# Router-table writes spread over POOL's steps, weight pieces at other places, six score banks for the last batch

## The chip, the cores and the metric

The kernel runs on one core of one Trainium2 chip. The metric is the device time of one execution in microseconds (us). The engines are called PE (matrix multiplications), DVE (vector), ACT (scalar), POOL (GpSimd) and SP (which only issues transfers). They run side by side, each through its own list of instructions in order, and wait for each other by semaphores.

## The reference

A Flamingo block on 32 batches of 112 tokens, width 256. First a cross attention whose queries come from the normed tokens x, and whose keys and values come from 375 normed context rows and the 112 normed tokens themselves (487 keys, 16 heads of 64):

```python
q, kv = lat @ Wq, concat([ctx_norm, lat]) @ Wkv
attn = softmax(q k^T / 8);  x = x + tanh(g_xattn) * (attn @ v) @ Wout
```

Then a mixture of 8 experts on the layer-normed result, two experts a token, hidden width 1024:

```python
gate = softmax(xn @ gate_w);  two best, their scores normed to sum 1
h = gelu(xn @ w1[e] + b1[e]);  y = h @ w2[e] + b2[e]
x = x + tanh(g_ffn) * (score0 * y0 + score1 * y1)
```

## The kernel before

Products are made of float16 (or float32r) halves: a number is split into a high and a low part, and three products of parts stand for one. ACT writes the high part, DVE or POOL the low one.

**The attention part** is one long software pipeline over steps t (`STEPS`, from -24 to 275). A step works on one pair of heads; a batch has 8 steps (`NP`), so batch b starts at t = 8b, and j = t % 8 is the place in the batch. `PAIRS` is 256. In step t PE makes, where t is even, the scores of pairs t and t+1 (L1125) into four banks `scores_ps`, then the K and V projections of pair t+8 into the two banks `proj_ps` (L1107), then the product with V of pair t-4 (L1156). Before the scores of step t it waits until all pairs before t are exponentiated. DVE takes each score's row minimum (`shifted_minimum`, L864), ACT the exponential (L639, function `exponential`), which waits until POOL is done with the pair two before, since `p_f` has two buffers. ACT then makes the high part of p (`p_high_of`, L648) and POOL the low part (`p_low_of`, L510). SP transposes p by DMA. POOL does o_f (L530) and o_low (L516) for the attention output too.

**The later stages** of a batch (output projection `out` L1176, residual and statistics `x2`, `rstd2`, `xn`, router logits, `top` for MAX8, and by groups of batches `hot`, `share`, `prefix`, `rank`, `entry`) hang on fixed steps counted from the batch's first one (`USUAL`, `LATE` for batch 29, `EARLY` for 30 and 31). `GROUPS` says which batches are ranked together: 8, 8, 8, 4, 2, 1 and 1. When a group is ranked (`rank_entries`), POOL writes for each batch and each of a token's two experts one row set into a table in DRAM, an indirect DMA (L587). `entries_at` gives one batch, two writes, to each step from the group's `entry` step on. The first group's writes are in steps 89 to 96, the second's in 153 to 160, the third's in 217 to 224 and the fourth's in 249 to 252.

**Weight pieces.** The experts' weights are 32 pieces ("units") of 512 KB, four an expert. A piece is loaded by SP (`load_unit`), split by ACT (`unit_high_of`, L667) and DVE (`unit_low_of`, L906). `SPLITS` puts pieces 0 to 22 in steps 250, 252, 254 and 256 to 275, `BEFORE_TILES` has 23 to 25, `TILE_SPLITS` 26 to 31 in iterations -2 to 3 of the tile loop. `LOADS` loads the piece four further one step after each split, since a load waits until its slot's former piece is split. b2 (1 MB) is loaded in step 260.

**Before the tiles** DVE computes from the counts which tile belongs to which expert (`table_row`, sets `row_known`); POOL waits for this and for all table writes, then reads the table (L593); PE turns it, DVE copies it, and POOL gathers the first rows (L599).

**The tile loop** has 35 tiles of 256 rows. Iteration t makes on PE the hidden layer of tile t+1 (L1256), the transposes of tile t+2 (L1266), and y of tile t (L1280). The hidden layer of tile n < 8 waits until 4(n+1) pieces are split. DVE splits the hidden values (L1052, L1054), splits the transposed x (L1066, L1068), makes y (L1076), and then splits its weight pieces of this iteration. Last, sums are copied to the output.

Of the kernel before, what the change touches and what calls it, by code (L numbers as in the profile page):

```python
# [82 lines left out]
GROUPS = ((0, 8), (8, 16), (16, 24), (24, 28), (28, 30), (30, 31), (31, 32))  # L83
# [16 lines left out]
def entries_at(t):  # L100

    return [first + t - step_of("entry", last - 1) for first, last in GROUPS if 0 <= t - step_of("entry", last - 1) < last - first]
# [18 lines left out]
def program(nc, x, ctx_in, g_x, g_f, ln_m_g, ln_m_b, ln_l_g, ln_l_b, wq, wkv, wout, gate_w, w1, b1, w2, b2, out):  # L121
# [4 lines left out]
    with ExitStack() as st:  # L126
# [195 lines left out]

        def subtracted(b):

            return POOL_BASE + POOL_COUNT * (b + 1)
# [49 lines left out]
        def _(sp):  # L375
# [37 lines left out]
            for t in STEPS:  # L413
# [44 lines left out]
                if t in LOADS:  # L458
                    load_unit(LOADS[t])
# [4 lines left out]
            for u in LAST_LOADS:  # L464
# [11 lines left out]
        def _(pool):  # L476
# [42 lines left out]
            for t in STEPS:  # L519
# [60 lines left out]
                for ob in entries_at(t):  # L580
# [5 lines left out]
                    for k in range(TOPK):  # L586
                        pool.indirect_dma_start(table.rearrange("r (n w) -> (r n) w", w=2), bass.IndirectOffsetOnAxis(ap=place_i[0:LQ, ob, k:k + 1], axis=0),  # L587
                                                entry[0:LQ, ob, k], None).then_inc(entered, 16)
# [37 lines left out]
        def _(act):  # L626
# [6 lines left out]
            def exponential(p, h):  # L633
# [5 lines left out]
                act.activation(p_f[0:LQ, p % 2, h, 0:LK], scores_ps[n][0:LQ, 0:LK], ACT.Exp, bias=shift[0:LQ, p // 2 % 2, n:n + 1], scale=-1.0,  # L639
# [29 lines left out]
            for t in STEPS:  # L669
# [55 lines left out]
                if t in SPLITS:  # L725
                    unit_high_of(SPLITS[t])
# [5 lines left out]
            for t in range(-2, TILES + 1):  # L732
# [23 lines left out]
                if t in TILE_SPLITS:  # L756
                    unit_high_of(TILE_SPLITS[t])

        @block.vector
        def _(dve):  # L760
# [100 lines left out]
            def shifted_minimum(p, h):  # L861
                n = 2 * (p % 2) + h
                dve.wait_ge(scores_done, 2 * p + h + 1)
                dve.tensor_scalar(passed[0:LQ, n, 0:LK], scores_ps[n][0:LQ, 0:LK], P_SHIFT, None, ALU.add, ALU.min,  # L864
# [43 lines left out]
            for t in STEPS:  # L908
# [103 lines left out]
                if t in SPLITS:  # L1012
                    unit_low_of(SPLITS[t])
# [297 lines left out]
```

## Time and profile before

| | |
|---|---|
| runs of the kernel before | 1851.1, 1853.73, 1851.03 us, median 1851.1 |
| the profiled execution | 1851.1 us, its span 1849.4 us |
| mean granted clock of PE | 0.967 of full speed |
| busy: PE, DVE, ACT, POOL | 90%, 71%, 65%, 68% of the span |
| PE's clock in 40 slices of the span | 0.9 or more in nearly all, 6, 5 and 8 tenths in slices 30 to 32 |

Slices are 46 us wide. The attention part ends in slice 29, the slices 30 and 31 hold the last stages of the last batches and the reading of the table, and the tile loop fills the rest.

### The profile page before, as it was taken

The page shows a single profiled execution, that of the slowest core. Times are in us where ns is not written, and L with a number is a line of the kernel's source. Part 1 is how long each engine was busy: PE and PEld are TensorE (multiplying, and loading weights), DVE is VectorE, ACT ScalarE, POOL GpSimd, SP SyncE. Part 2 cuts the span into 40 slices and gives each one's busy share as a digit, 9 for nine tenths or more (in the row PEclk, how much of TensorE's full clock was granted, in tenths as well). Part 3 has the DMA queues.
Part 4 walks back from the last instruction along what each step waited for, and adds up shares of the span by engine and source line. Part 5 has one row for each costly group of instructions (what it writes and reads, how often), then busy time and mean ns, then how long its engine had stood idle before and what let it go on. Part 6 is the DMA issues. An engine that isn't in the chain of part 4 may idle for free. (4 is left out here: it accounts for less than half of the span.)

```text
span 1849.4 us, 42314 instructions
## 1 busy us (share of the span) xinstructions
PE 1670.0 (90%) x15044; PEld 1168.0 (63%) x15044; DVE 1307.3 (71%) x3059; ACT 1200.6 (65%) x2732; POOL 1259.7 (68%) x1350
## 2 busy tenths in 40 slices
PE   1899999999989999998999999999851899999995
PEld 0456666666655666665566666556541799999994
DVE  4677787777766877776677778677665676666662
ACT  2587777777767787776787777677753444444442
POOL 5377777877788877778877777886673355445542
PEclk9999999999999999999999999999965899999998
DMA  4177767677657677676676767555788133323334
GB/s 146 36 140 137 148 143 146 139 148 144 140 113 139 137 150 149 139 142 111 136 145 137 143 142 141 108 113 106 161 203 244 47 50 53 50 47 50 52 51 103
DMA packets 597544, 223.37 MB, mean 121 GB/s; under 512 B 535202, under 2 KB 587984, under 8 KB 596892
## 3 DMA queue, kind: packets, MB, share of 16 engines
q1 hardware_dynamic: 581804, 202.18, 52.1%
q0 software_dynamic: 15536, 18.49, 6.4%
q8 instruction: 126, 2.06, 0.5%
q14 instruction: 78, 0.64, 0.1%
HBM read 71.39 MB, written 20.76 MB: 50 GB/s over the span
## 5 line engine op out<-in xcount | busy, mean ns | idle before, releaser
L510 POOL TENSOR_TENSOR p_parts<-p_space,p_parts 112x487 f16<-112x487 f32 x512 | 559.8, 1117 | 167.3 <-ACT p_parts L648 166.8
L639 ACT ACTIVATE p_space<-scores_ps,shift 112x487 f32<-112x487 f32 x512 | 338.6, 665 | 46.4 <-POOL p_parts L510 44.5
L864 DVE TENSOR_SCALAR_CACHE_REDUCE passed<-scores_ps 112x487 f16<-112x487 f32 x512 | 308.6, 660 | 26.3 <-PE scores_ps L1125 25.9
L694 ACT ACTIVATE k_hi<-proj_ps 128x488 fp32r<-128x488 f32 x256 | 148.0, 578 | 256.3 <-PE proj_ps L1107 256.1
L939 DVE SCALAR_TENSOR_TENSOR v_sb<-proj_ps,v_sb 128x512 f16<-128x512 f32 (+1 forms) x256 | 176.9, 691 | 164.5 <-ACT v_sb L708 163.6
L648 ACT ACTIVATE p_parts<-p_space 112x487 f16<-112x487 f32 x512 | 276.3, 608 | 0.0
L744 ACT ACTIVATE o_space<-scores_ps,b_sb,undo 128x256 f32<-128x256 f32 x280 | 139.3, 560 | 206.3 <-PE scores_ps L1256 206.1
L615 POOL DMA_INDIRECT sums_dram<-pt_space,ot_space x70 | 117.5, 1679 | 183.7 <-ACT pt_space L754 170.2
L933 DVE TENSOR_TENSOR k_lo<-proj_ps,k_hi 128x488 fp32r<-128x488 f32 x256 | 169.6, 662 | 102.1 <-ACT k_hi L694 101.3
L1107 PE MATMUL proj_ps<-kv_hi,wkv_hi 128*128 128x488 f16 x512 | 192.3, 376 | 38.5 <-DVE v_sb L939 20.6
L1156 PE MATMUL pv_ps<-v_sb,pt_space 128*128 128x128 f16 x2048 | 218.1, 221 | 7.0 <-DVE o_space L985 6.0
L1107 PE MATMUL proj_ps<-wkv_hi,kv_hi 128*128 128x512 f16 (+1 forms) x512 | 196.5, 384 | 9.3 <-DVE v_sb L939 9.1
L1107 PE MATMUL proj_ps<-wkv_lo,kv_hi 128*128 128x512 f16 (+1 forms) x512 | 196.1, 383 | 0.0
L1107 PE MATMUL proj_ps<-wkv_hi,kv_lo 128*128 128x512 f16 (+1 forms) x512 | 196.0, 383 | 0.0
L1256 PE MATMUL scores_ps<-o_parts_space,arena 128*128 128x256 f16 x1680 | 191.9, 275 | 4.0 <-issue 2.2
L1107 PE MATMUL proj_ps<-kv_hi,wkv_lo 128*128 128x488 f16 x512 | 190.9, 373 | 0.0
L1107 PE MATMUL proj_ps<-kv_lo,wkv_hi 128*128 128x488 f16 x512 | 190.8, 373 | 0.0
L1280 PE MATMUL proj_ps<-arena,g_parts 128*128 x1680 | 189.0, 273 | 0.0
L1256 PEld LDWEIGHTS scores_ps<-o_parts_space,arena 128*128 x1680 | 165.6, 99 | 25.0 <-issue 4.7
L1280 PEld LDWEIGHTS proj_ps<-arena,g_parts 128*128 128x128 f16 x1680 | 164.4, 98 | 18.6
L708 ACT ACTIVATE v_sb<-proj_ps 128x512 f16<-128x512 f32 (+1 forms) x256 | 152.8, 597 | 15.7 <-PE proj_ps L1107 8.0
L1156 PEld LDWEIGHTS pv_ps<-v_sb,pt_space 128*128 128x128 f16 x2048 | 134.8, 99 | 36.9 <-issue 8.7
(218 smaller groups left out, 3552.5 us busy)
## 6 DMA issues: line engine op xcount, KB each, us to landing
w_part<-in_L_ffn_w_dram SPq DMA_DIRECT2D x64, 256.0 KB, 3.8
arena<-in_L_ffn_w_dram SPq DMA_DIRECT2D x28, 512.0 KB, 4.9
ctx_sb<-in_ctx_dram SPq DMA_DIRECT2D x32, 375.0 KB
pt_space<-p_parts SPq DMA_TRANSPOSE x256, 4.0
x_sb<-in_x_dram SPq DMA_DIRECT2D x32, 112.0 KB
res_sb<-in_x_dram SPq DMA_DIRECT2D x32, 112.0 KB, 5.2
sums_dram<-x_sb SPq DMA_DIRECT2D x32, 112.0 KB, 2.8
xn_dram<-xn_sb SPq DMA_DIRECT2D x32, 112.0 KB, 2.0
```

Source lines behind the costliest of these rows:

```text
L510: pool.tensor_tensor(p_parts[0:LQ, p % PS, h, 1, 0:LK], p_f[0:LQ, p % 2, h, 0:LK], p_parts[0:LQ, p % PS, h, 0, 0:LK], ALU.subtract).then_i ...
L639: act.activation(p_f[0:LQ, p % 2, h, 0:LK], scores_ps[n][0:LQ, 0:LK], ACT.Exp, bias=shift[0:LQ, p // 2 % 2, n:n + 1], scale=-1.0, accum_ou ...
L648: act.activation(p_parts[0:LQ, p % PS, h, 0, 0:LK], p_f[0:LQ, p % 2, h, 0:LK], ACT.Copy).then_inc(p_high, 1)
L694: act.activation(k_hi[:, j], ps[:, 0:LKP], ACT.Copy).then_inc(kq_high, 1)
L708: act.activation(v_sb[(b + 1) % 2][0:rows, c, 8 * half_:8 * half_ + 8, 0], ps[0:rows, :].rearrange("p (n d) -> p n d", d=DH), ACT.Copy, sc ...
L864: dve.tensor_scalar(passed[0:LQ, n, 0:LK], scores_ps[n][0:LQ, 0:LK], P_SHIFT, None, ALU.add, ALU.min, accum_out=shift[0:LQ, p // 2 % 2, n: ...
L933: dve.tensor_tensor(k_lo[:, j], ps[:, 0:LKP], k_hi[:, j].bitcast(F32), ALU.subtract).then_inc(kq_low, 1)
L939: dve.scalar_tensor_tensor(out=v_of(1), in0=ps[0:rows, :].rearrange("p (n d) -> p n d", d=DH), scalar=V_SCALE, in1=v_of(0), op0=ALU.mult, ...
L1107: last = nc.tensor.matmul(out, lhs(a, k), rhs(c, k), start=(n == 0), stop=(n == 3 * KD - 1))
L1156: last = nc.tensor.matmul(pv_ps[:, at:at + 128], block_of(0, c), v[:, c, n].rearrange("p a d -> p (a d)"), start=(c == 0), stop=(c == KT - 1))
L1256: last = nc.tensor.matmul(h_ps[m][:, c * ROWS:c * ROWS + ROWS], experts[:, bass.ds(e1, 1), at:at + 128].rearrange("p o f -> p (o f)"), (xt ...
L1280: last = nc.tensor.matmul(y_ps[s][:, r * D:r * D + D], g_parts[:, s, a, m, c * ROWS + r * 128:c * ROWS + r * 128 + 128], experts[:, bass.d ...
```

## The change

- Group sizes become 8, 8, 6, 3, 3, 2, 1, 1.
- Table writes go through a waiting list. Only steps with j = 3 or 7 take from it: one write before step 208, two from there on; from step 248 on every step takes up to four.
- Weight pieces: fewer in the steps (12, the first in step 256), 2 before the tiles, 18 in the tile loop, up to three an iteration. Loads follow. b2 is loaded after piece 17, and DVE waits for it only at the y of tile 0.
- In the last batch (pairs 248 to 255) the scores go round six banks, the two `proj_ps` ones being the third turn, and PE waits for the exponentials of the pair three before, not for all.

```diff
-GROUPS = ((0, 8), (8, 16), (16, 24), (24, 28), (28, 30), (30, 31), (31, 32))
+GROUPS = ((0, 8), (8, 16), (16, 22), (22, 25), (25, 28), (28, 30), (30, 31), (31, 32))
...
+def entry_turns():
+    turns, waiting, ready = {}, [], {step_of("entry", last - 1): range(first, last) for first, last in GROUPS}
+    for t in STEPS:
+        waiting += [(ob, k) for ob in ready.get(t, ()) for k in range(TOPK)]
+        room = (1 if t < 208 else 2) if t % NP in (3, 7) else 0
+        if t >= PAIRS - NP:
+            room = 4
+        turns[t], waiting = waiting[:room], waiting[room:]
+    return turns
...
-SPLITS = {PAIRS - 6: 0, PAIRS - 4: 1, PAIRS - 2: 2}
-SPLITS.update({PAIRS + n: 3 + n for n in range(20)})
-BEFORE_TILES = (23, 24, 25)
-TILE_SPLITS = {-2: 26, -1: 27, 0: 28, 1: 29, 2: 30, 3: 31}
-LOADS = {t + 1: u + 4 for t, u in SPLITS.items()}
-LAST_LOADS = (26, 28, 29, 30, 27, 31)
+SPLITS = {0: (0,), 2: (1,), 5: (2, 3, 4), 10: (5,), 11: (6,), 17: (7,), 18: (8, 9), 19: (10, 11)}
+SPLITS = {PAIRS + n: units for n, units in SPLITS.items()}
+BEFORE_TILES = (12, 13)
+TILE_SPLITS = {-2: (14,), -1: (15, 16), 0: (17, 18, 19), 1: (20, 21, 22), 2: (23, 24, 25), 3: (26, 27, 28), 4: (29, 30), 5: (31,)}
+LOADS = {t + 1: [u + 4 for u in units] for t, units in SPLITS.items() if t + 1 in STEPS}
+FIRST_LAST = 4 + 10
+LAST_LOADS = tuple(range(FIRST_LAST, 18)) + (28, 29, 30) + tuple(range(18, 28)) + (31,)
...
+        def score_bank(p, h):
+            turn = (p - LAST_PAIR) % 3 if p >= LAST_PAIR else p % 2
+            return proj_ps[h] if turn == 2 else scores_ps[2 * turn + h]
...
-                if t == PAIRS + 4:
+            for u in LAST_LOADS:
+                if u == 28:
                     sp.wait_ge(p_low, 2 * PAIRS)
                     sp.dma_start(b2_sb, b2.partition_broadcast(128)).then_inc(b2_loaded, 16)
...
-                for ob in entries_at(t):
+                for ob, k in ENTRY_TURNS[t]:
...
-                    if t >= 2:
+                    if 2 <= t <= LAST_PAIR:
                         pe.wait_ge(exp_done, 2 * t)
+                    if t == LAST_PAIR + 2:
+                        pe.wait_ge(kq_low, 10 * NB)
+                        pe.wait_ge(v_low, PAIRS)
                     for p in (t, t + 1):
+                        if p >= LAST_PAIR + 3:
+                            pe.wait_ge(exp_done, 2 * (p - 2))
...
                     if ob >= NB - 2:
-                        pe.wait_ge(kq_low, 10 * NB)
-                        pe.wait_ge(v_low, PAIRS)
+                        pe.wait_ge(exp_done, 2 * (LAST_PAIR + 6))
```

The spare copy that `shifted_minimum` writes goes to `w_part` for every other two pairs of the last batch.

## Rows read from the trace of the kernel before

**Rows 1.** The page's first part: busy us, share of the span, instructions.

```profile
PE 1670.0 (90%) x15044; PEld 1168.0 (63%) x15044; DVE 1307.3 (71%) x3059; ACT 1200.6 (65%) x2732; POOL 1259.7 (68%) x1350
```

**Rows 2.** Stretches of one batch: start:end, length, busy of PE, PEld, DVE, ACT, POOL; clock; DMA.

```profile
463.66:504.58 40.92, 40.61 (x380) 26.79 (x377) 32.05 (x82) 30.90 (x75) 32.25 (x37) 1.00 0.66 140
504.58:551.37 46.79, 41.22 (x360) 25.54 (x358) 31.92 (x87) 31.26 (x74) 39.08 (x44) 0.96 0.57 107
551.37:596.40 45.03, 41.03 (x360) 25.62 (x358) 31.26 (x79) 31.16 (x74) 36.34 (x42) 0.96 0.75 143
596.40:635.60 39.20, 38.89 (x361) 25.03 (x358) 30.31 (x78) 30.80 (x74) 30.68 (x36) 1.00 0.71 144
...
833.83:879.53 45.70, 41.01 (x361) 25.53 (x358) 31.82 (x87) 31.23 (x74) 38.69 (x43) 0.96 0.61 110
879.53:923.15 43.62, 39.22 (x360) 25.02 (x358) 30.04 (x78) 31.01 (x74) 36.54 (x43) 1.00 0.66 138
...
1159.31:1205.78 46.47, 41.98 (x367) 26.29 (x366) 31.91 (x87) 31.92 (x75) 39.12 (x44) 0.96 0.60 110
1205.78:1250.02 44.24, 41.46 (x364) 26.43 (x362) 32.14 (x85) 31.00 (x74) 37.16 (x43) 0.96 0.54 104
```

**Rows 3.** Timeline at step 89: start, us, engine, what, [idle before and its releaser].

```profile
514.11 1.21 POOL L587 DMA_INDIRECT table_dram<-entry,place_i  x1 [2.33 <-DVE entry L900]
515.62 0.95 POOL L587 DMA_INDIRECT table_dram<-entry,place_i  x1 [0.30 <-issue]
516.60 2.19 POOL L510 TENSOR_TENSOR p_parts<-p_space,p_parts 112x487 f16<-112x487 f32 x2
518.88 0.67 ACT L639 ACTIVATE p_space<-scores_ps,shift 112x487 f32<-112x487 f32 x1 [3.06 <-POOL p_parts L510]
```

**Rows 4.** Two stretches right after it, columns as in rows 2.

```profile
520.00:521.20 1.20, 0.30 (x1) 0.11 (x2) 1.04 (x2) 1.08 (x4) 1.20 (x2) 0.91 1.04 196
521.20:522.40 1.20, 1.20 (x4) 0.44 (x3) 0.52 (x2) 0.76 (x2) 1.04 (x3) 0.50 0.95 185
```

**Rows 5.** Timeline of POOL in an undisturbed batch, the p_low after steps 3 and 7.

```profile
652.95 2.19 POOL L510 TENSOR_TENSOR p_parts<-p_space,p_parts 112x487 f16<-112x487 f32 x2 [2.21 <-ACT p_parts L648]
...
673.43 2.20 POOL L510 TENSOR_TENSOR p_parts<-p_space,p_parts 112x487 f16<-112x487 f32 x2 [1.09 <-ACT p_parts L648]
```

**Rows 6.** The line of the table writes: ns min/median/max on POOL.

```profile
L587 POOL DMA_INDIRECT table_dram<-entry,place_i x64: 938/947/3558, 514.1 to 1418.1; - x64
```

**Rows 7.** Timeline of the last batch.

```profile
1342.65 1.77 POOL L587 DMA_INDIRECT table_dram<-entry,place_i  x1 [0.16 <-issue]
...
1348.17 2.19 POOL L510 TENSOR_TENSOR p_parts<-p_space,p_parts 112x487 f16<-112x487 f32 x2
...
1350.45 0.67 ACT L639 ACTIVATE p_space<-scores_ps,shift 112x487 f32<-112x487 f32 x1 [5.09 <-POOL p_parts L510]
```

**Rows 8.** Last output projection: timeline, then its transposes' line.

```profile
1381.16 0.50 SPq L462 DMA_DIRECT2D p_space<-in_L_ffn_b_dram  x1
...
1390.31 0.39 PE L1176 MATMUL proj_ps<-wout_hi,ot_space 128*128 128x256 f16 x1 [9.45 <-DMA ot_space<-o_parts_space]
...
DMA to landing us min/median/max: 4.2/4.4/8.5
```

**Rows 9.** Timeline of the last batch's router.

```profile
1401.69 0.91 PE L1191 MATMUL proj_ps<-gate_sb,xnt_sb 128*112 128x8 f32 x4 [0.45 <-ACT xnt_sb L688]
...
1407.36 0.17 DVE L1006 MAX8 max_v<-proj_ps 112x8 f32<-112x8 f32 x1
...
1414.84 2.93 POOL L587 DMA_INDIRECT table_dram<-entry,place_i  x1 [9.88 <-DVE entry L900]
```

**Rows 10.** The chain of waits before the tiles: start, us, what.

```profile
1419.81 4.50 issue
...
1424.55 6.86 DMA ot_space<-table_dram,table_row
```

**Rows 11.** Timeline of the tile loop's start and of an iteration with one piece.

```profile
1440.20 8.23 PE L1256 MATMUL scores_ps<-o_parts_space,arena 128*128 128x256 f16 x48 [1.80 <-DVE o_parts_space L1068]
...
1473.26 0.75 DVE L1076 SCALAR_TENSOR_TENSOR pt_space<-proj_ps,undo,p_space 128x512 f32<-128x512 f32 x1 [1.45 <-PE proj_ps L1280]
1473.93 1.28 DVE L906 SCALAR_TENSOR_TENSOR arena<-wout_lo,scale_i,arena 128x1024 f16<-128x1024 f32 x1
...
1475.62 0.49 DVE L1052 TENSOR_SCALAR g_parts<-o_space,scale_i 128x512 f16<-128x512 f32 x1 [0.41 <-ACT o_space L744]
```

More of the change, by code:

```diff
@@ L97, in groups_at @@
     return [n for n, (first, last) in enumerate(GROUPS) if step_of(stage, last - 1) == t]
[L100 to L102 removed]
+def entry_turns():
[7 more added lines that the diff above has]
+    return turns
+ENTRY_TURNS = entry_turns()
 PART_STEPS = sorted([NP * b + 5 for b in range(28)] + [NP * b + 1 for b in (4, 8, 12, 16)])
 CHAIN = NP * 28
[L108 to L113 removed]
+SPLITS = {0: (0,), 2: (1,), 5: (2, 3, 4), 10: (5,), 11: (6,), 17: (7,), 18: (8, 9), 19: (10, 11)}
[5 more added lines that the diff above has]
+LAST_LOADS = tuple(range(FIRST_LAST, 18)) + (28, 29, 30) + tuple(range(18, 28)) + (31,)
 def part_of(part):
@@ L321, in program, with passed_of @@
         POOL_BASE, POOL_COUNT = 19, 4
+        LAST_PAIR = PAIRS - NP
+        def score_bank(p, h):
+            turn = (p - LAST_PAIR) % 3 if p >= LAST_PAIR else p % 2
+            return proj_ps[h] if turn == 2 else scores_ps[2 * turn + h]
+        def passed_of(p, h):
+            n = 2 * (p % 2) + h
+            spare = w_part[:, :, :].rearrange("p a n -> p (a n)").bitcast(F16).rearrange("p (s n) -> p s n", s=4)
+            return (spare if p >= LAST_PAIR and p // 2 % 2 == 1 else passed)[0:LQ, n, 0:LK]
         def subtracted(b):
@@ L457, in _ @@
                         load_unit(u)
-                if t in LOADS:
-                    load_unit(LOADS[t])
-                if t == PAIRS + 4:
+                for u in LOADS.get(t, ()):
+                    load_unit(u)
+            for u in LAST_LOADS:
+                if u == 28:
                     sp.wait_ge(p_low, 2 * PAIRS)
                     sp.dma_start(b2_sb, b2.partition_broadcast(128)).then_inc(b2_loaded, 16)
-            for u in LAST_LOADS:
                 load_unit(u)
@@ L585, in _ @@
                     pool.wait_ge(rank_done, n + 1)
-                    for k in range(TOPK):
-                        pool.indirect_dma_start(table.rearrange("r (n w) -> (r n) w", w=2), bass.IndirectOffsetOnAxis(ap=place_i[0:LQ, ob, k:k + 1], axis=0),
-                                                entry[0:LQ, ob, k], None).then_inc(entered, 16)
+                    pool.indirect_dma_start(table.rearrange("r (n w) -> (r n) w", w=2), bass.IndirectOffsetOnAxis(ap=place_i[0:LQ, ob, k:k + 1], axis=0),
+                                            entry[0:LQ, ob, k], None).then_inc(entered, 16)
             pool.wait_ge(row_known, 1)
@@ L724, in _ @@
                     act.activation(ratio[0:LQ, 1, 0:last - first], ratio[0:LQ, 0, 0:last - first], ACT.Exp).then_inc(shared, 1)
-                if t in SPLITS:
-                    unit_high_of(SPLITS[t])
+                for u in SPLITS.get(t, ()):
+                    unit_high_of(u)
             act.wait_ge(o_high, PAIRS // 2)
@@ L755, in _ @@
                         last.then_inc(y_weighed, 1)
-                if t in TILE_SPLITS:
-                    unit_high_of(TILE_SPLITS[t])
+                for u in TILE_SPLITS.get(t, ()):
+                    unit_high_of(u)
         @block.vector
@@ L1011, in _ @@
                     choose(n)
-                if t in SPLITS:
-                    unit_low_of(SPLITS[t])
+                for u in SPLITS.get(t, ()):
+                    unit_low_of(u)
             HS = slice(0, HALVES)
@@ L1077, in _ @@
                                              in1=b2_sb[:, bass.ds(e0, 1), :].broadcast_to((128, 2, D)), op0=ALU.mult, op1=ALU.add).then_inc(y_ready, 1)
-                if t in TILE_SPLITS:
-                    unit_low_of(TILE_SPLITS[t])
+                for u in TILE_SPLITS.get(t, ()):
+                    unit_low_of(u)
         @block.tensor
@@ L1124, in _ @@
                                 rows = slice(64 * h, 64 * h + 64)
-                                last = nc.tensor.matmul(scores_ps[2 * (p % 2) + h][0:LQ, 0:LKP], qq[rows, p % NP], kk[rows, p % NP], start=(n == 0), stop=(n == 2))
+                                last = nc.tensor.matmul(score_bank(p, h)[0:LQ, 0:LKP], qq[rows, p % NP], kk[rows, p % NP], start=(n == 0), stop=(n == 2))
                                 if n == 2:
```

7 lines of the change are left out of this document (4 added, 3 removed).

## The prediction

> **What bounds the kernel now.** The page first: PE is busy for 1670.0 of 1849.4 us, while POOL, DVE and ACT have 30% of their time free [rows 1]. So time can be won only where PE waits. The profiled execution took 1851.1 us, which is also the median of the three runs, so the sum below is made against 1851.1; 1.7 us of it lie around the span.
>
> Then the span in stretches of one batch (8 steps, from one even step's first score matmul to that of 8 steps later). An undisturbed batch takes 39.20 us, with PE busy 38.89 of them and the granted clock at 1.00 (2.4 GHz). The pairs of batches in which a group's table writes are issued take 46.79 and 45.03, 45.70 and 43.62, 46.47 and 44.24 us, POOL's busy time rises there from 30.7 to 36.3 to 39.1, and the clock falls to 0.96 in four of the six [rows 2]. Above 39.20 that is 7.59 + 5.83 + 6.50 + 4.42 + 7.27 + 5.04 = 36.7 us. The timeline at step 89 shows how: two writes of 1.21 and 0.95 us stand ahead of p_low of pair 88 (L510), which starts at 516.60; the exponential of pair 90 on ACT has then waited 3.06 us for POOL, and ACT's copy of V, which frees a projection bank, is queued behind it [rows 3]. PE has 1 matmul in 520.0 to 521.2 and then runs at a granted 0.50 (1.2 GHz) [rows 4].
>
> Last the stretch between the last full batch and the tile loop, by timeline and chain of waits: PE starts the first tile at 1440.20 [rows 11], 111.6 us after the scores of step 248 (1328.56), and in this stretch it mostly waits.
>
> **Part 1: table writes one by one.** By the new turns the 16 writes of the first group go one each to steps 91, 95, ... 151, those of the second to 155 ... 207 and two at 211; then two at a time at 215, 219, ... 247 (18 writes). Nothing is dropped: 64 writes as before. What hides them is POOL's idle time in odd steps: before p_low it waits 2.21 us after step 3 of a batch and 1.09 us after step 7 [rows 5]. A write costs 0.94 to 0.97 us of POOL (median 0.947) and 0.16 to 0.30 of issue [rows 3, 6], some 1.2 us. In a step 3 a single one is free; in a step 7 it runs over by some 0.15 us. A double one takes 1.2 + 1.2 = 2.4: over by 0.2 in a step 3, by 1.3 in a step 7. There are five double steps 7 (215 to 247): at most 5 x 1.3 = 6.5 us, at least 0. In rows 3 POOL's delay of some 3.3 us cost ACT 3.06 and PE about 2.3, so roughly 0.6 to 1 us of it was slack; I take 0.4 each, 2 us together. The single ones at step 7 (15 turns x 0.15 = 2.3 at most) I take as 0.
>
> What stays of the 36.7: the ranking on DVE at the end of a group (about 0.5 each, 1.5), the peak chain of steps 224 to 233 (0.8), and one more group end, as the third group is cut into 6 and 3 batches. A group end with eight batches costs 40.92 - 39.20 = 1.7 us [rows 2]; the matmuls there go with the batches of the group, so I take 1.0 (bounds 0 and 1.7). Sum: 36.7 - 2 - 1.5 - 0.8 - 1.0 = **31 us less** (bounds: 36.7 when nothing remains, and 36.7 - 6.5 - 2.3 - 1.5 - 2 - 1.7, about 22).
>
> **Part 2: last batch.** POOL is the bound: ACT's exponential of pair 252 waits 5.09 us for p_low of 250, which started only at 1348.17, after five and a half microseconds of writes from 1342.65 on [rows 7]. So the six score banks and the finer waits, which let PE run scores 250 to 255 up to two pairs earlier, are worth about 0 alone (0 to 2 us). Writes: before, eight in this stretch (2.3 + 5.5 + 3.0 = 10.8 us of POOL); after, six, four of them in step 249 (4.9 us ahead of p_low of 248, where two took 2.3) and two in 250. Following the loop p_low(p-2), exp(p), p_high, p_low(p) with the durations 2.19, 1.3 and 0.6, I get p_low of 255 done at 1367.3 instead of 1369.7: 2.4 us. The weight pieces 3 to 9, which stood between the last sums on DVE, ACT and POOL, are gone from steps 257, 259 and 260: another 2.5.
>
> The transposes for the last output projection land 8.5 us after their issue, where the median of this line is 4.4: the 1 MB of b2 was issued 0.6 us ahead of them [rows 8]. b2 is moved behind the piece 17: 3.5 us less. So the projection of batch 31, at 1390.31, comes 2.4 + 2.5 + 3.5 = 8.4 us earlier.
>
> From there to the last table write it was 24.5 us. The router's logits started at 1401.69 and were done by 1402.6; MAX8 came at 1407.36, because DVE stood at a weight piece that waited for its load; the write started at 1414.84 [rows 9]. After, only pieces 5 and 6 lie in steps 263 to 272, both loaded long before. Instruction by instruction (projection 5.0, x2 and statistics 1.2, rank of batch 30 1.4, xn 0.4, transposes 0.6, copy 0.4, logits 0.9, pieces 5 and 6 some 1.7 in the open, max 0.6, choose 0.9, prefix 0.9, rank 1.4, issue 0.3, semaphores 0.5) this is 16.2: 8.3 us less.
>
> From the write to the first tile it was 1414.84 to 1440.20, 25.4. Five pieces (7 to 11) and the slot arithmetic now stand on DVE ahead of the table read, 5 x 1.28 + 1.8, and piece 11 is loaded only after piece 7: some 9.5 us, about what the last writes and their landing take (1414.84 to 1424.55). The read then took 6.86 us beside weight loads [rows 10]; after, pieces 12 to 17, b2 and 28 to 30 fall into it again. I take 1 us more (bounds -3 and +6). Sum of part 2: 8.4 + 8.3 - 1 = **16 us less** (8 to 21).
>
> The Trainium skill, "DMA: Bandwidth & Descriptors", section "Issuing engines are not separate DMA queues", says that DMAs of all issuing engines end on the same 16 engines and interleave. That speaks against the new place of b2; the trace agrees with it (8.5 against 4.4 us), and this is rival A.
>
> **Part 3: tile loop.** 18 pieces are split in it instead of 6. PE is the bound at 10.91 us a tile. In an iteration with one piece (1.28 us) DVE idles 1.45 us before y and 0.41 before the first split of the hidden layer [rows 11], with one more wait of 0.43 some 2.3 us. Two more pieces are 2.56: 0.3 us too much in each of four iterations, against some 0.8 us of slack ahead of the copied x. I take 0.5 (0 to 2.5). The last piece, 31, stands on DVE after y of tile 5, and PE's next matmul, the hidden layer of tile 7's turn, waits for it: 0.67 + 1.28 + 0.2 = 2.15 us of open wait that was not there. If it drops the clock as in rows 4, 3 us at half clock add 1.6. I take **3 us more** in all (bounds 1.5 and 6.5).
>
> **Sum.** 1851.1 - 31 - 16 + 3 = 1807 us.
>
> **Rivals.** *A, the end gives its gain back.* b2 and 2.5 to 4 MB of pieces meet the table read and the first gather, and DVE becomes the bound of tiles 0 to 4. For: rows 8 and 10. Against: the same loads were there before. Part 2 shrinks to 6, part 3 grows to 6: 1851.1 - 31 - 6 + 6 = 1820. *B, idle time bounds nothing, so it isn't idle.* POOL's 1.09 us in step 7 is the slack of the loop p_low, exp, V copy; if each of the 20 turns in step 7 costs PE a wait and a spell of half clock as step 89's pair did (4.0 us), it is 1807 + 20 x 4.0 = 1887, slower. It decides from 2.2 us a turn. For: step 89 shows the price for 3.3 us of delay. Against: the overrun is 0.15 us in 15 of the turns. *C, the bursts aren't the writes.* The excess is ranking and group ends, which stay, so part 1 is 10 only: 1828. Against: POOL's busy time rises by just the writes, and the releaser is POOL. *D, it nets to nothing*: parts hidden by something that I don't see, 1850.
>
> **Chances.** Forecast 0.68 (its own range 1798 to 1815), A 0.17, C 0.09, D 0.02, B 0.04. Two in ten are left out by 1797 to 1821. What a measurement of this kernel can tell from no change is about 0.2%, 3.7 us: faster 0.94, within 0.02, slower 0.04.
>
> **What would show it.** Batches 88 to 104 at 39 to 40 us with POOL near 33 busy and clock 1.00; the batches at 216 and 232 at 40 to 41; the projection of batch 31 about 8 us sooner after step 248 and the first tile 95 us after it; one wait of some 2.2 us for DVE's last piece between tiles 5 and 6. It is wrong if writes in step 7 leave PE gaps, if the table read starts more than 11 us after the last ranking, or if tiles 0 to 4 take over 11.5 us.

## The result, and the profile after

| | before | after |
|---|---|---|
| median, us (4 runs each) | 1852.41 (1851.03 to 1855.10) | 1823.41 (1821.99 to 1825.22) |
| profiled execution, its span | 1851.1, 1849.4 | 1821.99, 1820.3 |
| mean granted clock | 0.967 | 0.975 |

The ratio is 0.984, with a 95% interval of [0.9824, 0.9855]: 29 us faster. The forecast was 1807, 44 us faster, with 1797 to 1821 as its range; the result lies 2.4 us outside. The direction was right; the gain is a third smaller than forecast.

The page's first part of the changed kernel shows where the time came from: PE, DVE, ACT and POOL are busy about as long as before [rows 1], so it is waiting that went.

```profile
PE 1663.3 (91%) x15046; PEld 1165.6 (64%) x15046; DVE 1316.1 (72%) x3073; ACT 1199.0 (66%) x2733; POOL 1255.9 (69%) x1350
```

Stretches of one batch as in [rows 2], for the changed kernel (columns as there): steps 88, 152, 216, 224, 232 and 240. All are cut at the first score matmul of the step.

```profile
502.44:544.26 41.82, 39.06 (x360) 25.11 (x358) 33.10 (x87) 30.80 (x73) 31.04 (x36) 1.00 0.61 127
...
821.35:863.18 41.83, 39.06 (x360) 25.10 (x358) 33.11 (x87) 30.80 (x73) 31.03 (x37) 1.00 0.68 129
...
1141.52:1182.47 40.95, 40.08 (x368) 25.75 (x366) 32.39 (x84) 31.03 (x74) 35.27 (x40) 1.00 0.69 135
1182.47:1224.86 42.39, 39.98 (x365) 25.63 (x363) 33.71 (x94) 31.01 (x73) 34.52 (x40) 1.00 0.56 107
1224.86:1268.88 44.02, 39.34 (x360) 25.03 (x358) 35.23 (x77) 31.14 (x73) 30.36 (x35) 1.00 0.52 103
1268.88:1308.40 39.52, 38.76 (x360) 24.96 (x358) 26.51 (x70) 30.07 (x72) 27.57 (x31) 1.00 0.67 135
```

The stretches of [rows 2] are cut 0.76 us later, at the step's second pair, all but the start of the one from 1159.31, which is a first pair's. Cut alike, its 46.47 us is 45.71, and the excess that the forecast sums to 36.7 is 35.9.

The clock is at 1.00 in every stretch, where five of the six in [rows 2] had 0.96 (the forecast's text says four of the six; the rows show five). But a group's end still costs: 41.82 and 41.83 us where 39.20 is undisturbed, and 44.02 in the stretch from step 232, which is a new excess.

By the first score matmuls of PE the whole difference of the profiled spans splits so (us, before to after, beside the forecast):

| part | before | after | change | forecast |
|---|---|---|---|---|
| start to the first scores | 74.7 | 73.4 | -1.3 | 0 |
| first scores to those of step 248 (part 1) | 1253.8 | 1235.0 | -18.8 | -31 |
| from there to the first tile (part 2) | 111.6 | 95.9 | -15.8 | -16 |
| first tile to the end (part 3) | 409.2 | 416.0 | +6.8 | +3 |
| sum | 1849.4 | 1820.3 | -29.1 | -44 |

So part 2 came as forecast, part 1 brought 12 us less, and part 3 cost 4 us more. (The profiled executions of e5 to e9, whose edits leave part 2 alone, have 95.7 to 98.0 us there, so about 2 us of that row can be chance.)

**Where part 1 stays.** The timeline of DVE in step 153 of the changed kernel, the end of the second group (start, us, engine, line, operation), has the ranking whole; the K copy that PE waits for is behind it.

```profile
828.76 0.21 DVE L912 TENSOR_TENSOR place<-tail_ps,base 112x64 f32<-112x64 f32 x1
...
829.90 0.16 DVE L918 TENSOR_SCALAR ratio<-ratio 112x8 f32<-112x8 f32 x1
830.10 0.20 DVE L919 RECIPROCAL ratio<-ratio 112x8 f32<-112x8 f32 x1
830.34 0.81 DVE L920 TENSOR_SCALAR entry<-ratio,tanh_g 112x8 f32<-112x8 f32 x1
831.06 1.15 DVE L921 SCALAR_TENSOR_TENSOR entry<-ratio,tanh_g 112x8 f32<-112x8 f32 x1
832.13 0.65 DVE L954 TENSOR_TENSOR k_lo<-proj_ps,k_hi 128x488 fp32r<-128x488 f32 x1
```

The same moments on POOL and on PE:

```profile
829.99 2.19 POOL L532 TENSOR_TENSOR p_parts<-p_space,p_parts 112x487 f16<-112x487 f32 x2 [0.69 <-ACT p_parts L669]
...
832.84 0.38 PE L1129 MATMUL proj_ps<-kv_hi,wkv_hi 128*128 128x488 f16 x1 [1.66 <-DVE k_lo L954]
```

From L912 to the end of L921 it is 3.45 us for nine operations on at most 128 elements a partition. Two of them stand out: L920 has 8 elements and takes 0.81 us, L921 has 8 and takes 1.15. POOL's p_low (two instructions in one row, from 829.99 to 832.18) runs just then, and L921 ends at 832.21, with it. In the profile of before the same two operations took 0.21 to 0.23 us each at all seven group ends (L899, L900 there), and POOL was then always idle. [rows 3] show why at the first: POOL's next instruction was the write that waits for this very ranking (2.33 us, for L900), and p_low stood behind it. Now the write comes steps later and p_low is free to run beside the ranking. PE loses 1.66 us in this gap. At the ends in steps 90 and 202 both operations are held too (0.81 and 1.15, 0.90 and 1.15 us); at the one in step 226 L920 is done before p_low is far (0.23) and only L921 is held (1.16).

The largest case comes at the end of step 231. The timeline of DVE, then of POOL:

```profile
1224.79 5.16 DVE L861 SCALAR_TENSOR_TENSOR peak_e<-peak_e 128x1 f32<-128x1 f32 x1
1229.98 0.68 DVE L945 SCALAR_TENSOR_TENSOR q_lo<-proj_ps,undo,q_hi 128x448 fp32r<-128x448 f32 x1
```

```profile
1222.77 1.01 POOL L608 DMA_INDIRECT table_dram<-entry,place_i  x1 [0.20 <-issue]
1224.09 0.94 POOL L608 DMA_INDIRECT table_dram<-entry,place_i  x1 [0.30 <-issue]
1225.05 2.20 POOL L532 TENSOR_TENSOR p_parts<-p_space,p_parts 112x487 f16<-112x487 f32 x2
1227.20 0.61 POOL L552 TENSOR_TENSOR o_space<-o_space,inv_sum 112x256 f32<-112x256 f32 x1
1227.77 2.16 POOL L532 TENSOR_TENSOR p_parts<-p_space,p_parts 112x487 f16<-112x487 f32 x2
```

One element a partition took 5.16 us: it ends at 1229.95, when POOL's unbroken run of operations ends at 1229.93. All of DVE is queued behind it, among it the row minima of the next scores. The kernel before had the same run of POOL at this place, also without a pause:

```profile
1248.05 2.20 POOL L510 TENSOR_TENSOR p_parts<-p_space,p_parts 112x487 f16<-112x487 f32 x2 [1.10 <-ACT p_parts L648]
1250.19 0.63 POOL L530 TENSOR_TENSOR o_space<-o_space,inv_sum 112x256 f32<-112x256 f32 x1
1250.77 2.19 POOL L510 TENSOR_TENSOR p_parts<-p_space,p_parts 112x487 f16<-112x487 f32 x2
...
1249.21 1.05 DVE L840 SCALAR_TENSOR_TENSOR peak_e<-peak_e 128x1 f32<-128x1 f32 x1
```

There the operation began 1.16 us into the run and ended with the first p_low. What the double write changed is where POOL's run stands against it: now it begins 0.26 us before the run, beside the second write, and ends with the run. In all eight traces in which the writes are spread and this operation has both inputs in SBUF it took 5.15 to 5.18 us.

**Part 2**, by the row of the last output projection, the last write, and the chain of waits (start, us, what):

```profile
1361.49 0.40 PE L1203 MATMUL proj_ps<-wout_hi,ot_space 128*128 128x256 f16 x1 [2.98 <-DMA ot_space<-o_parts_space]
```

```profile
1376.65 5.32 POOL L608 DMA_INDIRECT table_dram<-entry,place_i  x1 [2.99 <-DVE entry L921]
```

```profile
1388.49 6.90 DMA ot_space<-table_dram,table_row
...
1404.27 6.77 PE scores_ps L1283 x48
...
1411.47 3.32 issue
1414.79 8.30 PE scores_ps L1283 x48
```

The projection comes 53.1 us after the scores of step 248 (before 61.8 [rows 8]: 8.7 less, forecast 8.4); the wait for its transposes is 2.98 us where it was 9.45. To the first write of the last group it is 15.2 us (before 24.5 [rows 9]; forecast 16.2), and from there to the first tile 27.6 (before 25.4; forecast 26.4). The last two rows are already part 3: a pause of 3.32 us, after which tile 1's hidden layer takes 8.30 us, where 5.24 is the time at 2.4 GHz (5.4 in the timeline).

**Part 3**: ACT's row of piece 28, the last split of iteration 3, then DVE's row of piece 31 and PE's row at tile 7's hidden layer:

```profile
1465.48 1.15 ACT L688 ACTIVATE arena<-wout_hi,scale_i 128x1024 f16<-128x1024 f32 x1 [4.46 <-DVE arena L927]
```

```profile
1485.77 1.28 DVE L927 SCALAR_TENSOR_TENSOR arena<-wout_hi,scale_i,arena 128x1024 f16<-128x1024 f32 x1
```

```profile
1487.19 3.01 PE L1283 MATMUL scores_ps<-o_parts_space,arena 128*128 128x256 f16 x26 [2.46 <-DVE arena L927]
```

By the intervals from one hidden layer's first matmul to the next one's: the first two are 10.52 + 13.81 us, where before they were 10.91 + 10.93 (+2.5); the one with ACT's wait, tile 5 to 6, is 11.83 (+0.9); the one with piece 31, tile 6 to 7, is 14.01 (+3.1). The rest are 10.91 or 10.92, as before.

### The profile page after: what moved, and what is told of

It is laid out like the page before. It is cut to its first block and busy times, and to the rows that moved or that the text cites. A ratio compares the mean times of both kernels' runs of the same rounds, so it can differ in the third digit from the quotient of the medians.

```text
span 1820.3 us, 42338 instructions
## 1 busy us (share of the span) xinstructions
PE 1663.3 (91%) x15046; PEld 1165.6 (64%) x15046; DVE 1316.1 (72%) x3073; ACT 1199.0 (66%) x2733; POOL 1255.9 (69%) x1350
## 5 line engine op out<-in xcount | busy, mean ns | idle before, releaser
L885 DVE TENSOR_SCALAR_CACHE_REDUCE passed<-scores_ps 112x487 f16<-112x487 f32 x502 | 302.3, 659 | 24.6 <-PE scores_ps L1153 24.5
L1129 PE MATMUL proj_ps<-kv_hi,wkv_hi 128*128 128x488 f16 x512 | 191.5, 374 | 36.7 <-POOL kv_lo L559 13.5
```

The source lines that it names most:

```text
L885: dve.tensor_scalar(passed_of(p, h), score_bank(p, h)[0:LQ, 0:LK], P_SHIFT, None, ALU.add, ALU.min, accum_out=shift[0:LQ, p // 2 % 2, n:n ...
L1129: last = nc.tensor.matmul(out, lhs(a, k), rhs(c, k), start=(n == 0), stop=(n == 3 * KD - 1))
```

## The experiments

All ratios are against runs of the kernel before that were taken beside the experiment's; their medians were 1850.9 us (e1 to e4), 1852.7 (e5 to e8), 1851.4 (e9 to e11) and 1851.0 (e12, e13). "After" in the text is the changed kernel, 0.984. Differences from it in us are between medians; by the ratios they come out up to 3.4 us otherwise, so small ones are read from the traces. There stretches and steps are again cut at the step's first score matmul.

### Three parts, each alone, and the group sizes

First the change was taken apart. Only the waiting list of writes, with the old groups, on the kernel before:

```diff
+def entry_turns(): ...
...
-                for ob in entries_at(t):
+                for ob, k in ENTRY_TURNS[t]:
```

> The kernel before with the new table-write turns alone; groups, weight pieces and score banks as before. Theory W (the write bursts cost what they delay, the rest of the old excess is ranking on DVE, which stays): stretches at 504 and 551 fall to some 42.5 and 39.7 us, POOL idle runs hide the single writes; the third group's 16 writes then go two at a time at steps 219 to 247. From the first scores to those of step 248 it takes some 19 us less than before (1253.1 there), in all about 19 us less: 1833. Theory R (all of the old excess was the writes, and the change's shortfall comes from the extra group ends): the stretches fall to 39.5 to 40 us and the whole to about 1820.

Measured: 1829.8 us, ratio 0.9879 [0.9857, 0.9901]. From first scores to those of step 248 it takes 1231.4 us, 22.4 less than before (theory W: 19 less). The bursts are the writes, so rival C in the form "the bursts aren't the writes" is out. But the steps after a ranking are still long (12.8 us each at steps 90, 154 and 218, where 10.15 is undisturbed), and step 232 takes 13.1: the remainder is there with this edit alone.

Only the other places of the weight pieces and of b2:

```diff
-SPLITS.update({PAIRS + n: 3 + n for n in range(20)})
...
+SPLITS = {0: (0,), 2: (1,), 5: (2, 3, 4), 10: (5,), 11: (6,), 17: (7,), 18: (8, 9), 19: (10, 11)}
...
```

> The kernel before with the new places of the weight pieces and of b2 alone. Theory E (the time between the last batch's scores and the first tile is won by the pieces' and b2's places): first tile some 13 us sooner after the scores of step 248 (111.6 us before, 95.1 in the changed kernel), tile loop 4 to 7 us longer than 409.2, net 7 to 9 us less: about 1844. Rival F (it is won by fewer table writes in the last batch): the first tile only 3 to 5 us sooner, net nothing or slower: 1852 to 1855.

Measured: 1842.28 us, 0.9955 [0.9937, 0.9972]: 8 to 9 us less, as theory E said. The first tile comes 96.6 us after the scores of step 248, 15 us sooner than before, and the tile loop takes 415.9 us, 6.7 more. The two ratios multiply to 0.9834, the whole of what the change brings.

Only the six banks and the finer waits:

```diff
+            turn = (p - LAST_PAIR) % 3 if p >= LAST_PAIR else p % 2
+            return proj_ps[h] if turn == 2 else scores_ps[2 * turn + h]
...
```

> The kernel before with the six score banks and finer waits of the last batch alone. Theory P (POOL's low parts bound the last batch): no change, within 2 us of before, ACT still waits some 5 us for POOL once. Rival S (the scores' wait for all exponentials bounds it): 4 to 8 us less.

Measured: 1852.5 us, 1.0006 [0.9994, 1.0018]. Nothing, as forecast.

The changed kernel with the old group sizes:

```diff
-GROUPS = ((0, 8), (8, 16), (16, 22), (22, 25), (25, 28), (28, 30), (30, 31), (31, 32))
+GROUPS = ((0, 8), (8, 16), (16, 24), (24, 28), (28, 30), (30, 31), (31, 32))
```

> The changed kernel with the old groups (8, 8, 8, 4, 2, 1, 1). One group end less before step 248 (some 2.6 us for its ranking and 1.3 for its prefix matmuls), but two more table writes in step 250 and the eight-batch ranking in place of the six. Theory G (an extra group end costs what its DVE chain costs): the stretch up to step 248 is 3 to 4 us shorter, the last batch 2.5 us longer, so within 2 us of the changed kernel (1823.4). Rival H (the ranking costs by batches, not by group ends): stretch up to step 248 the same, so 2 to 3 us slower than the changed kernel.

Measured: 1820.43 us, 0.9834 [0.9812, 0.9857], 3 us better than after by the medians and 1 by the ratios; the intervals overlap, so it is no proof. Its parts: 3.6 us less in the attention (one group end fewer there), as theory G said, 3.9 more up to the first tile, and 2.7 less at tile 1, whose clock didn't fall in this trace (intervals 10.70 + 10.94). The forecast's 1.0 for the extra group end was too low, and the new sizes give as much in the last stretch as they take.

### What the remainder in the attention is

The product on the peak, with its input taken from the PSUM bank where it already stands:

```diff
+then(dve.scalar_tensor_tensor(out=peak_e[:, 6:7], in0=tail_bank[:, 480:481], scalar=float(D), in1=peak_e[:, 6:7], ...))
 dve.sem_inc(f_moved, 1)
-then(dve.scalar_tensor_tensor(out=peak_e[:, 6:7], in0=peak_e[:, 4:5], scalar=float(D), in1=peak_e[:, 6:7], ...))
```

> The changed kernel, but the one-column DVE operation of the peak chain at step 231 (scalar_tensor_tensor on peak_e, 5.16 us in the changed kernel's trace, 1.05 in that of before) reads one of its two inputs from PSUM, not both from SBUF. Theory L (DVE with two SBUF inputs is shut out while POOL's run of p_low, o_f, p_low holds the port; the double write at step 231 put that run just ahead of it): the operation takes 0.2 to 0.3 us, step 232 falls from 12.29 to some 8.5 us, the whole by 3.5 us: 1820. Rival M (the double write's delay of p_low alone makes the 12.29): the operation may get short, but step 232 stays above 11 us and the whole within 1 us.

Measured: 1819.36 us, 0.9823 [0.9806, 0.9839], 4 us better than after. Its timeline of DVE, and POOL's p_low beside it:

```profile
1224.10 0.16 DVE L860 SCALAR_TENSOR_TENSOR peak_e<-tail_ps,peak_e 128x1 f32<-128x1 f32 x1
1225.85 0.68 DVE L945 SCALAR_TENSOR_TENSOR q_lo<-proj_ps,undo,q_hi 128x448 fp32r<-128x448 f32 x1 [1.59 <-ACT q_hi L703]
...
1224.48 2.19 POOL L532 TENSOR_TENSOR p_parts<-p_space,p_parts 112x487 f16<-112x487 f32 x2
```

0.16 us instead of 5.16; step 232 goes from 12.29 to 8.74 us and its stretch from 44.02 to 40.49. So the stall of this operation was the cost, and not the double write's delay of p_low (rival M). That its two SBUF inputs were the cause is likely, but e5 alone doesn't prove it, since the edit also put the operation ahead of a semaphore signal: it starts 0.38 us before p_low, not 0.26, and is over when p_low starts. For the inputs speaks q_lo, of the same kind and with one input in PSUM: 448 elements take 0.68 us in the middle of p_low, as long as with POOL idle (0.68 in after, at 1229.98).

The ranking cut in two and moved to steps 2 and 4 after its own, for the first four groups (`finish_places`, `finish_scores` hold its second part):

```diff
+                    if deferred(n) and since == 2:
+                        finish_places(n)
+                    if deferred(n) and since == 4:
+                        finish_scores(n)
...
```

> The changed kernel, but for the first four groups only the two DVE operations that free the PSUM bank stay at the ranking's step (j = 0); the rest of the places goes two steps later, the scores' part four steps later, where DVE has idle gaps of about 0.9 us. Same instructions. Theory N (what stayed of the old excess is the ranking's chain on DVE ahead of the K and V low parts): the steps after the rankings (12.78, 12.04, 12.78 and 13.17 us) fall to 10.2 to 11.2, the whole by 6 to 8 us: 1816. Rival O (it is the transfers or the prefix matmuls of a group end): those steps stay within 0.5 us, the whole too.

Measured: 1813.74 us, 0.9793 [0.9776, 0.9809], 9.7 us better than after. Two stretches of its trace, steps 88 and 96 (columns as in [rows 2]), then the two operations of the scores at their new place:

```profile
505.56:544.74 39.18, 38.87 (x361) 25.02 (x359) 33.02 (x87) 30.80 (x73) 29.87 (x35) 1.00 0.65 135
544.74:584.47 39.73, 39.02 (x362) 25.09 (x360) 31.35 (x80) 30.80 (x73) 33.05 (x38) 1.00 0.79 153
```

```profile
530.74 1.29 DVE L941 TENSOR_SCALAR entry<-ratio,tanh_g 112x8 f32<-112x8 f32 x1
531.95 0.66 DVE L942 SCALAR_TENSOR_TENSOR entry<-ratio,tanh_g 112x8 f32<-112x8 f32 x1
```

The excess after a ranking is gone (39.18 us where after has 41.82; the next batch keeps its 39.7; steps 90, 154, 202 and 226 take 10.15 or 10.16), though the two operations are still shut out, for 1.29 and 0.66 us: at this place it costs no time. By the trace the gain lies in the attention: 1225.9 us from the first scores to those of step 248, 9.1 less than after, and 95.7 from there to the first tile (after: 95.9). The peak's stall is still there, so its step 232 stays at 12.29 us.

The opposite: two operations of the ranking's middle made three times, four small operations more at the same four ends:

```diff
+                if last <= 25:
+                    f_then(... picked ...)
+                    f_then(... rank ...)
...
```

> The changed kernel, with the product and the sum of the ranking (two of its eight DVE operations) made three times for the first four groups; same result. The two take some 0.65 us for eight batches and 0.45 for three in a chain. Theory N (DVE's chain sets the step): the four steps after the rankings grow by 0.9 to 1.4 us each, the whole by 4 to 5 us: 1828. Rival O: within 1 us.

Measured: 1827.59 us, 0.9869 [0.9853, 0.9886], 4.2 us worse, as theory N said. Steps 90, 154, 202 and 226 grew by 0.8, 1.5, 0.7 and 1.2. At the first three the scores' two operations, pushed behind p_low's end, took 0.23 us each instead of 0.81 to 0.90 and 1.15, so part of what four operations more cost was won back: length counts, and the shutting out counts, and the two trade. PE's gap was the same at steps 90 and 154 (2.42 and 2.43 us, after 1.66), but in step 154 the mean granted clock was 0.88 and in step 90 1.00, which is the other 0.8 us of that step.

To tell these two apart, tanh(g_ffn) was taken out of the scores and multiplied into the weight column once before the tiles; the second score is 1 minus the first. This leaves two operations with a single input where there were three with up to three:

```diff
-f_then(dve.reciprocal(ratio[0:LQ, 0, 0:n], ratio[0:LQ, 2, 0:n]))
-dve.tensor_scalar(entry[..., 0, 1], ratio[0:LQ, 0, 0:n], tanh_g[0:LQ, 1:2], None, ALU.mult)
-dve.scalar_tensor_tensor(out=entry[..., 1, 1], in0=ratio[0:LQ, 0, 0:n], scalar=tanh_g[0:LQ, 1:2], in1=ratio[0:LQ, 1, 0:n], ...)
+f_then(dve.reciprocal(entry[..., 0, 1], ratio[0:LQ, 2, 0:n]))
+dve.tensor_scalar(entry[..., 1, 1], entry[..., 0, 1], -1.0, 1.0, ALU.mult, ALU.add)
...
-dve.tensor_copy(weight[:, :], tail_bank[:, 128:128 + HALVES])
+dve.tensor_scalar(weight[:, :], tail_bank[:, 128:128 + HALVES], tanh_g[:, 1:2], None, ALU.mult)
```

> The changed kernel, with the last part of the ranking of every group written without a second input from SBUF: the score is 1/(1+r) and 1 - 1/(1+r) (both of one input), and tanh(g_ffn), which both were multiplied by, is multiplied into the weight column once before the tiles. One small operation of DVE fewer a group, all else where it was. In the changed kernel these two operations (L920, L921) took 0.81 and 1.15 us at the first three group ends, while p_low (two inputs from SBUF) ran on POOL, and ended with it; with POOL idle they take 0.23 and 0.22. Theory S (the ranking costs what it does because POOL shuts its last two operations out): they take some 0.2 each also beside p_low, the V and K copies behind them start 1.5 us sooner, PE's gap of 1.66 us after the ranking is under 0.4, the steps at 90, 154, 202 and 226 fall from 12.0 to 13.2 us to 10.6 to 11.6, and the whole is 5 to 7 us below the changed kernel: 1817. Theory N (the length of the chain of small operations, each with its wait, sets it): one operation of eight is gone, 0.15 us at each of four ends; the steps stay above 11.9 and the whole is within 1.5 us of the changed kernel: 1822.5.

Measured: 1816.68 us, 0.9809 [0.9796, 0.9823], 6.7 us better than after, where S said 1817 and N 1822.5. The timeline of DVE, of POOL and of PE at the end of the second group:

```profile
829.34 0.20 DVE L919 RECIPROCAL entry<-ratio 112x8 f32<-112x8 f32 x1
829.58 0.81 DVE L920 TENSOR_SCALAR entry<-entry 112x8 f32<-112x8 f32 x1
830.30 0.66 DVE L952 TENSOR_TENSOR k_lo<-proj_ps,k_hi 128x488 fp32r<-128x488 f32 x1
```

```profile
829.23 2.19 POOL L532 TENSOR_TENSOR p_parts<-p_space,p_parts 112x487 f16<-112x487 f32 x2 [0.69 <-ACT p_parts L669]
```

```profile
831.01 0.38 PE L1127 MATMUL proj_ps<-kv_hi,wkv_hi 128*128 128x488 f16 x1 [0.60 <-DVE k_lo L952]
```

The number is S's, its reason only in part. One operation of a single SBUF input, L920, still takes 0.81 us beside p_low, so "two inputs" is not the whole condition; the reciprocal beside the same p_low takes 0.20. The gain is that one shut-out operation stands there instead of two: L920 ends at 830.39, about where the first of POOL's two instructions ends (829.23 plus half of 2.19 is 830.33), and PE's gap is 0.60 us instead of 1.66. Steps 90, 154 and 202 go from 12.8 to 11.73 us each. Step 226 stays at 12.43: there after had only one shut-out operation, 1.16 us, and e12 has one too, L920 with 1.01. That is 3.2 us for the three steps, and the attention is 3.5 shorter; the rest of the 6.7 (5.7 by the ratios) isn't located, so S's total came out partly by luck.

The Trainium skill, "SBUF — State Buffer", section "SBUF: two separate sides", has a wider condition: a port pair is shared by VectorE and GpSimd and held exclusively for a whole instruction, against a VectorE operation with two SBUF inputs (where the GpSimd one reads SBUF), or one in a two-port fast mode. The traces agree in kind: 5.16 against 0.16 us with the input in PSUM, and 0.81 us for the float32 SBUF-to-SBUF TENSOR_SCALAR, which would be the fast-mode case. But the 5.16 us span five instructions of POOL, not one. That the fast mode is what holds L920 is the Trainium skill's word; no run here switched it off.

### The tile loop, and b2

Piece 31 in the iteration of 29 and 30:

```diff
-4: (29, 30), 5: (31,)}
+4: (29, 30, 31)}
```

> The changed kernel, with piece 31 split in iteration 4 of the tile loop (29, 30, 31) and not in iteration 5. Theory K (PE waits 2.45 us for it between tiles 5 and 6): the tile of 14.01 us falls to 10.9, one neighbour may grow by at most 0.5, whole 2.5 to 3 us less: 1820.6. Rival: DVE is full in iteration 4, so the wait only moves: within 1 us.

Measured: 1820.41 us, 0.9831 [0.9815, 0.9848], 3.0 us better than after (1.7 by the ratios). DVE's three splits now stand together, and tile 7's hidden layer behind them starts without a wait (timelines of DVE and PE):

```profile
1474.66 1.27 DVE L927 SCALAR_TENSOR_TENSOR arena<-wout_lo,scale_i,arena 128x1024 f16<-128x1024 f32 x1
...
1477.05 1.28 DVE L927 SCALAR_TENSOR_TENSOR arena<-wout_hi,scale_i,arena 128x1024 f16<-128x1024 f32 x1
```

```profile
1484.35 5.40 PE L1283 MATMUL scores_ps<-o_parts_space,arena 128*128 128x256 f16 x48
```

The intervals tile 5 to 6 and 6 to 7 are 11.97 + 11.43 us, where after has 11.83 + 14.01: 2.4 less. Of the eight traces in which piece 31 has its late place, five (e2, e4, e6, e11, e12) show a further loss that after's doesn't: PE's wait of 2.23 to 2.38 us is followed by a hidden layer of 7.08 us instead of 5.4, and the interval tile 7 to 8 is 12.59 instead of 10.92, with a granted clock of 0.86. None of the four with the piece moved (e8, e9, e10, e13) shows it. Row of e4:

```profile
1483.67 7.08 PE L1283 MATMUL scores_ps<-o_parts_space,arena 128*128 128x256 f16 x48 [2.23 <-DVE arena L927]
```

b2 back at step 260, ahead of the last transposes, the rest as changed:

```diff
+                if t == PAIRS + 4:
+                    sp.wait_ge(p_low, 2 * PAIRS)
+                    sp.dma_start(b2_sb, b2.partition_broadcast(128)).then_inc(b2_loaded, 16)
```

> The changed kernel with b2's load at its old place (step 260), just ahead of the transposes of the last output projection. Theory T (the transposes wait behind 1 MB on the same DMA engines): they land after some 8 us and not 3.6, the projection and the whole come 3 to 4 us later: 1827. Rival (the write of the table and its read gain as much, since b2 no longer meets them): within 1 us.

Measured: 1823.7 us, 0.986 [0.9842, 0.9879]: above after by 0.3 us by the medians and by 3.7 by the ratios, whose intervals overlap. The times don't decide between theory T and its rival. The row of the projection in its trace:

```profile
1364.01 0.39 PE L1203 MATMUL proj_ps<-wout_hi,ot_space 128*128 128x256 f16 x1 [6.13 <-DMA ot_space<-o_parts_space]
```

The wait for the transposes is 6.13 us where it was 2.98, and all traces with b2 moved have 2.9 to 3.0 there, so the term exists at the projection. How much of it reaches the end stays open: the projection is 1.9 us later after step 248 (55.0 against 53.1) and the first tile 1.5 (97.4 against 95.9), but e5 to e9, which leave this part alone, spread over 52.2 to 54.8 and 95.7 to 98.0.

### Repairs together

Deferred ranking, peak from PSUM and piece 31 with 29 and 30 (the three edits above):

> The changed kernel with the three edits together: peak operation with an input from PSUM, ranking later, piece 31 in iteration 4. If they are independent, 4 + 9.7 + 3 = 16.7 us less than the changed kernel: 1806.7. If ranking later already cured step 232 (its third group's rest also lies near the peak chain) less, 1810.

Measured: **1805.06 us**, 0.9756 [0.974, 0.9773]. It beats both kernels, 46 us below the one before; independent gains were to give 1806.7. Its stretches of steps 152, 224 and 232, where after has 41.83, 42.39 and 44.02:

```profile
818.87:858.05 39.18, 38.87 (x360) 25.04 (x358) 33.01 (x87) 30.78 (x73) 31.17 (x37) 1.00 0.71 138
1174.32:1214.83 40.51, 39.87 (x365) 25.64 (x363) 33.05 (x94) 30.78 (x73) 34.47 (x40) 1.00 0.58 112
1214.83:1255.43 40.60, 39.00 (x361) 25.11 (x360) 30.55 (x76) 30.79 (x73) 30.46 (x35) 1.00 0.56 111
```

The same with the old group sizes:

> The same with the old groups. With the ranking off the path, a group end costs only its prefix matmuls (1 to 1.7 us), so cutting the third group in two costs some 1.5 us before step 248 and saves 4.7 in the last batch (two table writes fewer in step 250): theory G' 2 to 4 us slower than the kernel with all three. Rival: a group end still costs 4 us, and this one is the same or 1 us faster.

Measured: 1807.81 us, 0.9767 [0.975, 0.9784], 2.8 above the one before it, with intervals that overlap. By the traces it is 0.5 us shorter in the attention and 3.4 longer from there to the first tile (100.6 against 97.2), some 3 in all, which is what theory G' said; but its clock also fell at tile 1 (10.52 + 13.83) and e9's didn't, another 2.5. So the new group sizes may be worth 3 us once the ranking is off the path; the times alone don't show it.

The scores without tanh, peak from PSUM and piece 31 with 29 and 30, the ranking where it was:

> The same, with the peak's product read from PSUM (as in e5) and piece 31 with pieces 29 and 30 (as in e8); the ranking itself stays in one step. Theory S: the three gains add up, 6 + 4 + 3 = 13 us below the changed kernel, 1810, near the kernel that defers the ranking (1805), since an unblocked ranking still leaves half a microsecond or so a group end. Theory N: 0.6 + 4 + 3, 1815.5.

Measured: 1810.37 us, 0.9778 [0.9764, 0.9791]: S's sum (1810) holds, and the gains add up. Deferring the ranking (e9) looks some 4 us better than shortening it, by ratios whose intervals just overlap.

## Why the prediction was right or wrong

**The failed step** is the one in part 1 that begins "What stays of the 36.7: the ranking on DVE at the end of a group (about 0.5 each, 1.5), the peak chain of steps 224 to 233 (0.8)". It was priced from the busy time of some small operations, without asking what stands behind them on DVE and what runs beside them on POOL. After the change, the steps behind the four rankings are 2.6 us (three times) and 2.3 us above their undisturbed 10.15, 10.2 us together, and step 232 is 4.1 above its 8.24: 14.3 where the forecast left 2.3 for both. That is the missing 12 us. e6 shows the first term (deferring takes it away), e7 and e12 show that both the chain's length and the operations shut out by POOL are in it, e5 shows the second. Rival C had half of this: its "the ranking stays" was true, its "not the writes" was not (e1).

**That undisturbed writes are free** held. In the stretches of single writes POOL is busy for 31 to 33 us, the clock is 1.00, and those between group ends take 39.2 us. Rival B is out. The double writes (2 us forecast, at most 6.5) cost little as writes: the steps behind them, 216, 224 and 240, are 1.0, 0.3 and 1.0 us above 8.24, and step 232 of e5 is 0.5 above. The one at step 231 cost the other 3.5 by where it put POOL's run against an operation of DVE, not through POOL's own lateness (e5).

**One more group end** (1.0, bounds 0 and 1.7): too low. The third and the fourth ranking of the changed kernel lie in the attention at 2.6 and 2.3 us; with the old sizes this part is 3.6 us shorter (e4), though as much is lost later.

**Part 2** (16, measured 15.8). Its parts, 8.4 and 8.3, came as 8.7 and 9.4, and "1 us more" up to the first tile as 2.3. The sum was right. Of its term for b2, 3.5 us, e11 shows 3.15 in the wait for the transposes and leaves open how much of it reaches the end. Six banks at nothing: right (e3). Rival A, by which the end gives its gain back, didn't happen: the table's read took 6.90 us, where it was 6.86 [rows 10].

**Part 3** (3 with bounds 1.5 and 6.5, measured 6.8). The wait for piece 31 came where it was forecast, at tile 7's hidden layer: 2.46 us of PE's wait for 2.15, and 3.1 in the interval, and its removal gave 3.0 in the whole (e8). The 1.6 us that it was to add by a dropped clock didn't come in after's trace, but came as 1.7 in five others (e8's text). The 0.5 for DVE came as 0.9 from another place, by the timeline ACT's wait for the slot of piece 28; this was not tested. What was not forecast is 2.5 us at tile 1: a pause of 3.32 us and then 8.30 us at the lower clock, where before a pause of 2.24 left it at 1.00. It varied from trace to trace: tile 1 to 2 took 10.9 us in before, e4, e6, e8 and e9, 12.2 to 12.6 in e1, e2, e3, e5, e7, e11, e12 and e13, and 13.8 in after and e10. e3 has the tile loop of before, and e1 and e5 had pauses of only 2.25 and 2.26 us, so neither the moved pieces nor the length of the pause explains it alone. Its cause stays open.

**The range** was too narrow. The bounds of the three parts alone (22, 8 and 6.5) would have reached 1828, and part 1 came out at 18.8, under its lower bound of 22: the cost of what stays was given one value and no bound above, where the other terms had two.

## What to carry to other kernels

When a burst on one engine is spread out, look at what else stands at the burst: the small serial work of the same moment (here a ranking of nine tiny operations on DVE) was hidden in the burst's shadow and is then on the path with its full length. A tiny DVE operation on SBUF data beside a long POOL operation can cost the POOL operation's rest, and everything behind it waits; look whether one input can come from PSUM, make such operations fewer, or put them into a step in which nothing waits for DVE. Price each thing that stays as carefully as what goes, with a bound above.

## What the runs showed of the hardware

- A DVE operation of one element a partition took 5.16 us while POOL ran five instructions without a pause (1225.05 to 1229.93), and it started 0.26 us before the first of these, beside the tail of an indirect write. In the ranking, L920 and L921 each ended with one of p_low's two instructions. In the kernel before the peak operation got in behind the first p_low of an equally unbroken run (1.05 us). So the blocked engine sometimes gets in between two operations of the other and sometimes not; what decides it was not tested.
- Which DVE operations are shut out: a SCALAR_TENSOR_TENSOR of 448 elements with one input in PSUM is not (0.68 us beside p_low, e5), a reciprocal from SBUF is not (0.20, e12), a float32 TENSOR_SCALAR from SBUF to SBUF is (0.81 instead of 0.17, e12), and so is a SCALAR_TENSOR_TENSOR with two SBUF inputs (1.15 instead of 0.22, after).
- Pauses of PE of like length had different effects on the granted clock: in e7 a gap of 2.42 us left it at 1.00 and one of 2.43 us was followed by a step at 0.88; before tile 1 a pause of 2.24 us left it at 1.00 in before, and after one of 2.25 us in e1 the hidden layer took 7.09 us instead of 5.4. The gaps of 1.66 us in after's attention left it at 1.00; the pause of 3.32 us before tile 1 did not.
